# Routing's two-operand steps leave VectorE, and a key tile's value products stand in two halves

## What is computed

```python
x = L0_attn_x                                   # (8, 1024, 128)
# 8 heads of 32: softmax attention over layernorm(x)
scores = einsum('bqhd,bkhd->bhqk', q, k) * scale
out = einsum('bhqk,bkhd->bqhd', softmax(scores), v)
x = x + out.reshape(b, t, 256) @ Wo.T
# 14 experts, two for each token
probs = softmax(layernorm(x) @ gate_w.T)
top2_p, top2_i = top_k(probs, 2)
w = top2_p / maximum(top2_p.sum(-1), 1e-10)
x = x + w[:, 0:1] * out0 + w[:, 1:2] * out1 ...  # rows of the two chosen experts
```

## Time and profile before

| | before |
|---|---|
| median of three runs | 2246.83 us |
| the profiled execution, its own time | 2234.0 us |
| its span in the trace | 2232.3 us |
| mean granted TensorE clock | 0.887 |
| busy: TensorE / VectorE / ScalarE / POOL | 1722.2 / 1527.5 / 1177.9 / 1366.9 us |
| the 64 heads in the trace | 175.7 to 1138.3 us |
| from the last head to the next stage | 1138.3 to 1237.3 us |

### The profile page before, as it was taken

One profiled execution on the slowest core, in us unless ns is written; L12 is line 12 of the kernel. 1 busy time (PEld: TensorE's weight loads), 2 busy tenths in 40 slices (PEclk: granted clock), 3 DMA queues, 4 the chain that ended last, 5 costly groups with the idle time before them and its releaser, 6 DMA issues. The chain is left out here.

```text
span 2232.3 us, 54806 instructions
## 1 busy us (share of the span) xinstructions
PE 1722.2 (77%) x18737; PEld 1007.6 (45%) x18737; DVE 1527.5 (68%) x3787; ACT 1177.9 (53%) x2275; POOL 1366.9 (61%) x1088
## 2 busy tenths in 40 slices
PE   7977999998989899898952799377767776100997
PEld 3423455444444444444432688344444443000897
DVE  5756888899889889888835234178888877620453
ACT  4625887877777677777741355224444444021343
POOL 0004777766778777777785233488888872155465
PEclk9977999999999999999975799688999988555999
DMA  4754222221313122222222434400000000132332
GB/s 154 247 170 139 60 69 79 59 81 55 93 57 95 58 72 79 60 90 62 78 78 76 156 125 122 152 21 20 19 19 19 19 19 0 43 114 77 99 102 63
DMA packets 161611, 178.39 MB, mean 80 GB/s; under 512 B 39905, under 2 KB 124776, under 8 KB 161416
## 3 DMA queue, kind: packets, MB, share of 16 engines
q1 hardware_dynamic: 146584, 145.41, 21.3%
q0 software_dynamic: 13824, 29.43, 4.0%
q10 hardware_dynamic: 1008, 0.92, 0.1%
HBM read 97.76 MB, written 78.16 MB: 79 GB/s over the span
## 5 line engine op out<-in xcount | busy, mean ns | idle before, releaser
L941 DVE TENSOR_REDUCE halfmax<-p_m 128x1 f32<-128x512 f32 x1024 | 657.5, 685 | 122.3 <-PE p_m L694 111.0
L922 ACT ACTIVATE probs<-p_s,ESCALE 128x512 f32<-128x512 f32 x1024 | 645.9, 689 | 103.8 <-PE p_s L718 84.5
L632 POOL TENSOR_TENSOR sum_p<-sum_p,probs 128x1024 f32<-128x1024 f32 x192 | 455.7, 2374 | 38.9 <-ACT probs L922 25.4
L694 PE MATMUL p_m<-ka,qa 96*32 96x512 f16 x4096 | 422.6, 396 | 40.2 <-DVE halfmax L941 26.3
L718 PE MATMUL p_s<-qa,ka 98*32 98x512 f16 x4096 | 417.5, 388 | 15.9 <-DMA qa<-max_lo 10.7
L725 PE MATMUL p_o<-probs,vh 128*32 128x256 f32 x4096 | 320.0, 384 | 0.4 <-ACT probs L922 0.4
L632 POOL TENSOR_TENSOR sum_p<-probs 128x1024 f32<-128x1024 f32 x64 | 151.6, 2369 | 217.9 <-ACT probs L922 217.5
L694 PEld LDWEIGHTS p_m<-ka,qa 96*32 96x32 f16 x4096 | 114.3, 95 | 302.8 <-DVE halfmax L941 247.5
L1653 PE MATMUL ln_p_cum<-ln_kv,c_tri 128*128 128x512 f32 (+1 forms) x384 | 169.8, 587 | 89.6 <-POOL ln_kv L1597 89.6
L1306 ACT ACTIVATE e_h<-e_p_h,e_w 128x256 f32<-128x256 f32 x316 | 126.8, 474 | 159.3 <-PE e_p_h L1285 85.3
L718 PEld LDWEIGHTS p_s<-qa,ka 98*32 98x32 f16 x4096 | 118.2, 97 | 112.0 <-ACT probs L922 25.3
(11 more groups left out here) (298 smaller groups left out, 2740.6 us busy)
## 6 DMA issues: line engine op xcount, KB each, us to landing
e_xb<-xs SPq DMA_DIRECT2D x40, 257.0 KB
e_xb<-xs SPq DMA_DIRECT2D x78, 128.0 KB, 2.0
ys<-e_y SPq DMA_DIRECT2D x78, 128.0 KB, 1.9
v<-pj_v SPq DMA_DIRECT2D x8, 1024.0 KB, 5.0
qa<-q SPq DMA_DIRECT2D x64, 128.0 KB
ka<-k SPq DMA_DIRECT2D x64, 128.0 KB
vh<-v SPq DMA_DIRECT2D x64, 128.0 KB
o<-ot SPq DMA_DIRECT2D x64, 128.0 KB
```

What stands on the lines that cost most here:

```text
L632: nc.gpsimd.tensor_tensor(sum_p[i][:, :], (sum_p[i] if n else probs[0])[:, :], probs[k][:, :], ALU.add).then_inc(sum_p_d, 1)
L694: mm = nc.tensor.matmul(max_bank(s, n)[j * DH0:(j + 1) * DH0, :], qa[s][0:KA, (n // 2) * P + j * DH0:(n // 2) * P + (j + 1) * DH0], ka[s][ ...
L922: nc.scalar.activation(probs[k][:, h * HALF:(h + 1) * HALF], score_bank(u % SLOTS, k, h)[:, :], ACT.Exp, scale=ESCALE[:, 0:1]).then_inc(pr ...
L941: nc.vector.reduce_max(halfmax[u % 2][:, n // 2, n % 2:n % 2 + 1], max_bank(u % SLOTS, n)[:, :], AX.X).then_inc(max_read, 1)
```

## The change

VectorE no longer multiplies the probabilities by the reciprocal of their total (the totals are kept for the end), no longer forms counts by tile, adds the expert's start inside TensorE's accumulation instead, and makes the masks in 16 steps with one scalar each; POOL adds the two masks; ScalarE copies indices, gates and the running base. Ranks stand in gap 10 and slots in gap 11, rows are sent one head earlier, and all gates are made in one go at the end of the stage. `values` is issued in two halves, each of two column groups, one behind each maximum. Batches 6 and 7 use `mark_experts` in place of the 16 steps.

```diff
@@ TensorE
-            def spread(u, col, lhs, rhs, start, stop):
-                for j in range(4):
+            def spread(u, col, lhs, rhs, start, stop, quarters=range(4)):
+                for j in quarters:
...
-            def values(u, k):
-                pe.wait_ge(probs_d, u * SCORES + 2 * k + 2)
+            def values(u, k, h):
+                pe.wait_ge(probs_d, u * SCORES + 2 * k + h + 1)
...
+                last = spread(u, 0, v[u % SLOTS][:, k, :], probs[k], k == 0, k == KT - 1, range(2 * h, 2 * h + 2))
+                if h:
+                    last.then_inc(pv_d, 1)
@@ key_tile, inside the loop over h
                         max_half(u + 2, 2 * k + h)
-                values(u, k)
+                    values(u, k, h)
@@ ranks (gap 10 in place of 11)
                 pe.wait_ge(hot_d, b + 1)
-                pe.wait_ge(seen_d, (b + 1) * ST)
-                nc.tensor.matmul(pos_ps, c["stri"][:, :], both[:, :, :], start=True, stop=False)
-                nc.tensor.matmul(pos_ps, c["ones"][:, :], seen[:, 0:ST, :], start=False, stop=True).then_inc(pos_d, 1)
+                from_first(pe, base_d, b)
+                nc.tensor.matmul(pos_ps, c["ident"][:, :], base[:, :].unsqueeze(1).broadcast_to([P, ST + 1, E0]), ...)
+                nc.tensor.matmul(pos_ps[:, 0:ST, :], c["stri"][:, :], both[:, :, :], ...)
+                for t in range(ST):
+                    mm = nc.tensor.matmul(pos_ps[:, t + 1:ST + 1, :], c["ones"][:, :], both[:, t:t + 1, :].broadcast_to([P, ST - t, E0]), ...)
+                mm.then_inc(pos_d, 1)
@@ POOL
+                if n == 0:
+                    pool.wait_ge(places, 2 * b + 2)
+                    nc.gpsimd.tensor_copy(slot[b % NX][:, :], tabs["slotf"][...]).then_inc(slot_d, 1)
...
+            def join_marks(b):          # in head 22 + 8b, behind its fourth sum
+                pool.wait_ge(marks_d, b + 1)
+                nc.gpsimd.tensor_tensor(both[:, :, :], hot[:, 0, :, :], hot[:, 1, :, :], ALU.add).then_inc(hot_d, 1)
@@ ScalarE
+            def keep_bests(b):          # index 1, behind key tile 6
+                act.wait_ge(choice, 2 * b + 2)
+                nc.scalar.copy(GATE[...], best[:, :, 0:2]).then_inc(gates_d, 1)
+            def keep_chosen(b):         # the same place
+                nc.scalar.copy(chosen[...], at[:, :, 0:2]).then_inc(chosen_d, 1)
+            def keep_base(b):           # index 4, behind key tile 6
+                act.wait_ge(pos_read, b + 1)
+                nc.scalar.copy(base[:, :], pos_ps[:, ST, :]).then_inc(base_d, 1)
...
+            keep_base(B - 3)            # behind the last head
             for b in range(B - 2, B):
                 roots(b)
@@ VectorE
+            nc.vector.tensor_copy(steps[:, :, 0], c["iota"][:, 0:E0])     # steps is [P, E0, 2]
+            def mark_chosen(b):
+                dve.wait_ge(chosen_d, b + 1)
+                for k in range(2):
+                    for t in range(ST):
+                        last = nc.vector.tensor_scalar(hot[:, k, t, :], steps[:, :, 0], chosen[:, k, t:t + 1], None, ALU.is_equal)
+                last.then_inc(marks_d, 1)
...
-            def count_tiles(b):
...
             def find_slots(b):
                 dve.wait_ge(pos_d, b + 1)
-                nc.vector.tensor_tensor(place[:, :, :], pos_ps, start[...], ALU.add).then_inc(pos_read, 1)
-                nc.vector.tensor_tensor(placed[...], hot[...], place[...], ALU.mult).then_inc(places, 1)
+                nc.vector.tensor_tensor(placed[:, :, :, :], hot[:, :, :, :], pos_ps[...], ALU.mult).then_inc(pos_read, 1)
@@ route
                     find_experts(b)
+                b = sequence(gap, 9)
+                if b is not None and b < B - 2:
+                    mark_chosen(b)
                 b = sequence(gap, 1)
                 if b is not None:
                     add_attention(b, 0)
...
                 b = sequence(gap, 11)
-                    count_tiles(b)
+                    find_slots(b)
@@ behind the last head
-            count_tiles(B - 3)
+            find_slots(B - 3)
             scales(B - 2)
-            find_slots(B - 3)
-            gates(B - 3)
...
             find_rows(nc, dve, tabs, E0, SLOT[:, :], found)
+            gates()
```

More of the change, by code:

```diff
@@ L457, in attend @@
         xT = sb("r_xT", [P, GT])
-        top, total, prob = sb("r_top", [P, G]), sb("r_total", [P, ST]), sb("r_prob", [P, ST, E0])
+        top, totals, sums, prob = sb("r_top", [P, G]), sb("r_totals", [P, TILES]), sb("r_sums", [P, TILES]), sb("r_prob", [P, ST, E0])
+        chosen, steps = sb("r_chosen", [P, 2, ST]), sb("r_steps", [P, E0, 2])
         best, at = sb("r_best", [P, ST, 8]), sb("r_at", [P, ST, 8], U32)
[L460 to L464, removed]
+        hot, both = sb("r_hot", [P, 2, ST, E0]), sb("r_both", [P, ST, E0])
+        now, start, base = sb("r_now", [P, E0]), sb("r_start", [P, E0]), sb("r_base", [P, E0])
+        placed = sb("r_placed", [P, 2, ST, E0])
         zeros = sb("r_zeros", [P, BT // P, D])
@@ L615, in scatter @@
             def scatter(h, half):
-                b = next((m for m in range(B) if 0 <= h - FIRST - 14 - m * H0 < H0), None)
+                b = next((m for m in range(B) if 0 <= h - FIRST - 13 - m * H0 < H0), None)
                 if b is None:
                     return
-                n = 2 * (h - FIRST - 14 - b * H0) + half
+                n = 2 * (h - FIRST - 13 - b * H0) + half
                 i, t, k = n // 8, n // 2 % G, n % 2
+                if n == 0:
+                    pool.wait_ge(places, 2 * b + 2)
+                    nc.gpsimd.tensor_copy(slot[b % NX][:, :], tabs["slotf"][:, b * ST * 2:(b + 1) * ST * 2]).then_inc(slot_d, 1)
                 apart(pool, slot_d, b + 1, passed)
@@ L637, in head @@
                         scatter(u, n - 2)
+                    marked = sequence(u, 10)
+                    if n == 3 and marked is not None and marked < B - 2:
+                        join_marks(marked)
             for s in range(SLOTS):
@@ L649, in _ @@
                 normalise(u)
-            for h in range(UNITS, FIRST + 14 + B * H0):
+            for h in range(UNITS, FIRST + 13 + B * H0):
                 for half in range(2):
@@ L854, in _ @@
             ranks(B - 1)
-            pe.wait_ge(pos_read, B)
-            pe.wait_ge(seen_d, B * ST + 1)
-            nc.tensor.matmul(p_r[:, 0:E0], c["ones"][:, :], seen[:, 0, :], start=True, stop=True).then_inc(count_d, 1)
         @block.scalar
@@ L904, in behind_tile @@
                         exponentials(b)
+                    b = sequence(h, 9)
+                    if b is not None:
+                        keep_bests(b)
+                        if b < B - 2:
+                            keep_chosen(b)
+                    b = sequence(h, 12)
+                    if b is not None:
+                        keep_base(b)
             act.sem_inc(od_d, OD0)
@@ new lines, in mark_experts @@
+            def mark_experts(b):
+                dve.wait_ge(best_d, b + 1 + (b - B + 2))
+                from_first(dve, pos_read, b)
+                for k in range(2):
+                    last = nc.vector.scalar_tensor_tensor(out=hot[:, k, :, :], in0=at[:, :, k].unsqueeze(2).broadcast_to([P, ST, E0]), scalar=1.0,
+                                                          in1=c["iota"][:, 0:E0].unsqueeze(1).broadcast_to([P, ST, E0]),
+                                                          op0=ALU.mult, op1=ALU.is_equal)
+                last.then_inc(best_d, 1)
+                dve.wait_ge(best_d, b + 2 + (b - B + 2))
+                from_first(dve, pos_d, b)
+                nc.vector.scalar_tensor_tensor(out=both[:, :, :], in0=hot[:, 0, :, :], scalar=1.0, in1=hot[:, 1, :, :],
+                                               op0=ALU.mult, op1=ALU.add).then_inc(hot_d, 1)
@@ L1074, in route @@
                     scales(b)
-                b = sequence(gap, 12)
-                if b is not None:
-                    find_slots(b)
-                b = sequence(gap, 13)
-                if b is not None:
-                    gates(b)
                 b = sequence(gap, 7)
```

122 lines of the change are left out of this document (57 added, 65 removed).

## The result

The forecast was 2208 us and a gain of 1.7%. The median of four runs of the changed kernel is 2273.64 us (2271.47 to 2276.6) against 2246.01 for the kernel before on the same chip (four runs, 2236.34 to 2247.13): a ratio of 1.0138, 95% interval 1.0105 to 1.0172. The range given (2186 to 2249) doesn't hold it. The profiled execution took 2272.18 us, its span is 2270.4 against 2232.3.

A forecast was written before the change was run, and what follows sets the result against it. TensorE was taken as the bound, VectorE close. Batches -41.3, last four heads +0.7, halves 0 and the end +1.6 gave -39.0 us, 2208 from the median 2246.83; range 2186 to 2249.

The forecast's parts named there:

- signs of being wrong: Forecast wrong if heads 20 to 59 take under 570 or over 605 us, or heads without routing move over 0.2.
- The pause of `ranks` goes: Head 40: `ranks` no longer waits for VectorE's counts; index 4 takes about 15.3 us at clock 1.00.
- The build-up of a batch: Eight heads: first batch's 112.65 us plus 1.9, 0.3 and 2.65 gives 117.5; five batches 587.5 against 628.78, -41.3 us.
- The masks' wait: Index 2: the first mask waits out POOL's sum, the other 15 follow at once; +2.65 us per batch.
- Rival C: Index 2: POOL and VectorE alternate at every mask, adding 5.65 us in six gaps, +33.9, 2242 us; chance 0.22.
- The halves: Value products, every tile: column groups run for themselves, nothing is lost; -0.02 to +0.02 us per tile, taken as 0.
- mirrored: Value products: maxima due at uneven distances before and after, only mirrored; taken as costing 0.
- Rival D: Value products: next scores wait for the half, 0.43 us in 512 tiles, +223, 2431 us; chance 0.07.
- Behind the last head: `keep_base(5)` delays the square root's table load, +0.5 us; chains of the last two batches +0.5 each; +1.6 in all.
- The sum: Whole kernel: -41.3 + 0.7 + 0 + 1.6 = -39.0 us on the profiled execution's 2234.0, which is 2195.
- The last step: Profiled execution is 12.8 us below the median 2246.83; the same -39.0 us from the median gives 2208 us.

The follow-up runs named there:

- e1: The changed kernel with the value products whole again, behind the second maximum; 2211.56 us, 1.0052 of the kernel before.
- e3: The changed kernel with whole value products and all masks made in one two-operand step of 224 elements; 2167.34 us, 0.9853 of the kernel before.
- e6: The kernel before, unchanged, run again for its trace on one of the later chips; 2200.0 us.
- e2: The kernel before with only the value products in halves of two column groups, one behind each maximum; 2220.40 us, 1.0097 of the kernel before.
- e7: The kernel before with value products in halves by columns, 128 columns of all four groups behind each maximum; 2195.0 us, 0.9977 of the kernel before.
- e8: The kernel before with whole value products behind the first maximum of a tile instead of the second; 2213.29 us, 1.0054 of the kernel before.
- e5: The changed kernel as it is, run again on one of the later chips; 2240.72 us, 1.0174 of the kernel before.
- e11: The changed kernel with one mask step, value products halved by columns, and ScalarE's `keep_base(5)` behind `roots(6)`; 2161.39 us, 0.9840 of the kernel before.
- e9: The changed kernel with whole value products and the 16 mask steps behind `add_attention` instead of ahead; 2200.24 us, 1.0007 of the kernel before.
- e12: The changed kernel with value products halved by columns and one mask step, placed behind `add_attention`; 2157.20 us, 0.9818 of the kernel before.

## Why the prediction was wrong

Both of its own signs of being wrong came: forty heads over 605 us (647.6), and heads without routing moved by over 0.2 us (0.50).

**The pause of `ranks` goes: right.** No row shows it waiting for VectorE any more. Head 40 takes 15.22 us in e1 at clock 1.00 (forecast 15.3), head 39 (index 3) 15.18, which is 1.75 above the first batch's head 15 (forecast 1.9 above), and the first batch 112.68 (112.65).

**The build-up of a batch: right on the later chips, short on the first.** With one mask step e3's forty heads take 581.1 us, 116.2 per batch, against a forecast of 117.5 with a mask wait of 2.65 (measured on TensorE 1.54, so 116.4). `ranks` with its new matmuls (L802, L804, L806) is busy for 16.3 us in six batches in after, 2.7 each, forecast 2.6. But the forty heads of before take 628.8 us on the first chip and 612.1 in e6, and those of after 647.6 and 631.5, while heads 12 to 19 take the same on both (before 112.65 and 112.67, after 116.04 and 116.03). So some 3.2 us per batch behind the first belong to that chip, in both kernels, by one trace of each. The forecast built all batches from the first one, and by that booked these 16 us as a gain.

**The masks' wait: the first step that failed.** The text took "1.6 + 1.2 + 0.1 = 2.9 us, less 0.2 slack", because two casts followed one another at once although a sum of POOL was queued. In after it is 6.2 us, and 2.1 us of slow clock besides (TensorE's busy time in e1's head 38, 16.98, against e3's 14.87). Both parts of the term were mis-sized. A POOL step that is queued gets its turn after a single mask step, and the casts were no evidence against that: the second had begun at 793.44, before POOL's sum began at 793.46. And a short step of this kind has a pitch of 0.137 us, not the casts' 0.08. Rival C, given 0.22, had both the sequence and the price right: it said one step at the end of the sum, one behind the multiplication, one behind the third sum and the rest in the scatter, and 117.5 + 5.65 = 123.15 us per batch; e1 measures 122.8.

The conditions that the Trainium skill gives for the two-port mode (VectorE: DVE Perf Modes, Mode 2×_2P) name no unit stride, so that the stride of `steps` would not free the masks. The trace agrees: in head 38 the first three take 1.42, 0.77 and 2.38 us behind POOL's steps.

**The halves: the second step that failed.** "If groups run for themselves, the other two go on with the next scores, and nothing is lost", with bounds of 0.02 us per tile. The condition holds and the conclusion doesn't: 13.25 less 12.75 us is 0.0625 us per tile, three times the bound. What was left out is that the banks are shared by all four groups: a lead of one pair is worth nothing to VectorE. That the division of the groups costs is shown by e2 against e7; how the cost comes about is argued. Also "mirrored" places were taken as equal; e8 shows that they aren't (+0.25 us per head). Rival D named the sign and a point of decision, 0.08 us per tile, but by another mechanism (a serial pass), which the starts at 307.03 and 307.32 exclude.

The strict order of starts that the Trainium skill (TensorE: Matmul & The Clock Gate, Part 3) states is again not what the trace shows: the leading pair's maximum starts at 307.03, ahead of the trailing pair's score at 307.10, which stands before it in the program.

**Behind the last head: the number came out by luck.** From the last head to the end of the span it is 1095.7 us (2270.4 - 1174.7) against 1094.0 (2232.3 - 1138.3): +1.7, forecast +1.6. But this stretch varies by more than that: it is 1077.0 us in e6 and 1082.1 in e7, which has the same program behind the last head, 1082.6 in e5 and 1077.9 in e1. The table load stands between `find_slots` and `scales`, as said; ScalarE, then VectorE:

```profile
1181.74 0.17 ACT L915 COPY r_base<-p_r 128x14 f32<-128x14 f32 x1 [7.00 <-DVE r_placed L1072]
1181.93 1.28 ACT L884 ACT_TABLE_LOAD   x1
```

```profile
1183.47 0.20 DVE L1019 RECIPROCAL r_rstd<-r_rstd 128x8 f32<-128x8 f32 x1 [1.27 <-ACT r_rstd L884]
```

Its price up to the normalised rows was 1.35 us (e11) where 0.5 stood; no run separates the other terms.

**The sum.** On the later chips, from e6 to e5: the routing with one mask step -32.3 us (e3 less e6), the 16 blocked steps +41.3, the halves +27.9, together +36.9 in the heads. Against the profiled execution on the first chip the forecast was 2195.0. With the 33.9 that rival C adds to the forecast's own wait, and the measured 27.9 for the halves and 16.1 for the chip, it would have been 2272.9; that execution took 2272.2. Two of these three terms were measured afterwards, so the agreement shows that the terms add up, not that they could have been forecast. The last step, adding the 12.8 us between the profiled execution and the median of before, had no ground: for after the two are 1.5 us apart, so the medians differ by 27.6 us where the profiled executions differ by 38.2. The chances were 0.22 for C and 0.07 for D, and no case joined a cost of the masks with a cost of the halves.

## What to carry to other kernels

Where VectorE's steps are held by GpSimd's, count a chain of VectorE steps by steps, not by elements: one step of 224 elements waited for one step of POOL (e3), sixteen of 14 for three (after), and a delay longer than the buffers in front of TensorE (here two banks, 1.4 us) reaches it in whatever order the rest stands. Moving the delaying step behind the one that TensorE waits for helps only if the delay fits into those buffers: it gained nothing in the forty heads with a delay of over 7 us (e9), and 8 us in five heads with one of 0.69 us (e12).

When TensorE's work is interleaved, divide it by columns and leave the column groups together, as long as a consumer waits for all groups of a bank. And when two edits are in one change, price their sum as a case of its own.

## What the runs showed of the hardware that was not expected

- VectorE and POOL took turns after each single step while both had one queued: three masks of 14 elements took 1.42, 0.77 and 2.38 us, each to within 0.03 us of the end of a POOL step. POOL's indirect DMA issue (1.01 us) didn't hold the masks up in after: 13 ran in 1.92 us across it. In e9, where a sum followed the issue at once, masks ran during its first 0.4 us, and the next one, begun 0.62 us before its end, lasted until the end of the sum (3.03 us). Whether the issue or the queued sum held it in those 0.62 us is open.
- The same `tensor_scalar` with an accumulated result isn't held: 0.17 us in the middle of a POOL sum, pitch 0.15 us with the instruction that reads the accumulator.
- Four column groups with equal work stay together (starts 0.22 us apart, four at a time); given unequal work, pairs were up to 0.29 us apart in their starts, and what is lost stands in no row of TensorE's waits.
- One chip took 2246 us for the kernel before and three others 2198 to 2201, with granted clocks of 0.887 and 0.890. Of the 34.0 us between the two profiled executions 18.9 are in heads 20 to 63 (684.9 against 666.0 us), none in heads 12 to 19, and 17 behind the last head (1094.0 against 1077.0); heads 0 to 11 took 2 less. The cause is open.
